# Deformable attention on one Trainium2 core: softmax per 512 queries, maximum subtracted in PSUM, other slots for the small stages

## The chip, the cores and the metric

The kernel runs on one NeuronCore of a Trainium2 chip (trn2). The metric is the device time of one execution in microseconds, here the median of three runs. Engines are named as in the profile: PE (TensorE matmul), PEld (its weight loads), DVE (VectorE), ACT (ScalarE), POOL (GpSimd) and SP (SyncE, which issues the DMAs).

## The reference

Two layers of a block with deformable attention run one after another on x of 2 x 128 x 32 x 32, fp32. Per layer and image:

- q is a grouped 1x1 convolution (8 heads of 16 channels). A 6x6 depthwise convolution with stride 4, gelu and a 1x1 product give 64 sampling positions per head; the image is sampled there bilinearly, and k and v come from the samples.
- The scores of a head are 1024 queries x 64 keys, with a learned bias: for each query and key the signed logarithm of their distance in x and y goes through a small network of 2 -> 32 -> 32 -> 1 with relu.
- softmax over the 64 keys, product with v, output projection and residual, then an MLP of 128 -> 512 -> 128 with gelu and a residual.

```
pos = grid_q[:, :, None, :] - grid_kv[:, None, :, :]
bias = jnp.sign(pos) * jnp.log1p(jnp.abs(pos))
bias = jax.nn.relu(bias @ cpb_w1 + cpb_b1)
bias = jax.nn.relu(bias @ cpb_w2 + cpb_b2)
bias = (bias @ cpb_w3 + cpb_b3).reshape(b, GROUPS, H * W, Hd * Wd)
sim = jnp.einsum('bhid,bhjd->bhij', qh, kh) + bias
attn = jax.nn.softmax(sim, axis=-1)
```

## The kernel before

The work is 4 segments (2 layers x 2 images), each of 4 units (pairs of heads; the 128 partitions are the 2 x 64 keys of a pair), each of 2 phases (512 queries), each of 8 steps. So there are 256 steps, 64 to a segment. The bias network is nearly all of the work.

In a step g, DVE makes the hidden layer for 16 keys x 512 queries (first_layer, L578, one 128x2048 maximum) into one of three buffers. PE does layer 2: 16 products of 32x32 tiles with the distance features (L785, bf16) and 16 with h (L790, fp32, two records each), into two pairs of PSUM banks. ACT applies relu to the two (relu2, L430). PE then does layer 3 of the step before: four products of 128x32 (L802, fp32) that accumulate into the phase's bank of scores. At the second step of a phase scores_start (L806 to L814) begins that bank with the query-key product, one 128x128 product of 512 columns (L812). PSUM holds a ring of three bank pairs, taken in turn by layer 2 and by the small stages, and two single banks of scores, one phase each.

The softmax of a unit, once both its phases are complete: copy_scores (L433, ACT) copies the scores with a bias into probs, per phase; scores_transpose (L884, PE) makes eight 128x128 transposes (L889); score_max (L700, DVE) takes the negative maximum over the 64 keys (L704); widen_max (L513, ACT) repeats it over 64 columns (L519); max_spread (L892, PE) turns it back with eight fp32r products (L896); max_off (L708, DVE) adds it to probs (L711); exp (L522, ACT) is taken in place (L524). Per segment, exp_sums and attend (L907, PE) follow, two DMA round trips and DVE's reciprocal (L715) for the sums, divide, project, residual1, mlp_up (L930) with gelu (L529), mlp_down (L940) and residual2 (L737).

The stages ahead of a segment's attention are norm1, q, the convolution (products on DVE and POOL, L310, sums, gelu), offset, tanh, positions, spread (L859), features, distances (L493, ACT), hats (L672, L675, DVE), hat_products (L681 on DVE, L410 on POOL), sample (L871) and keys_values. They run within the steps of the segment before.

What sets the order is written out by hand: BEFORE_SLOTS, AFTER_SLOTS and SOFTMAX_SLOTS give, for each engine and stage, the step after whose own work the stage is put into that engine's queue, counted from the segment's or unit's start. Each engine runs its queue strictly in order and waits on semaphores. Slots of AFTER_SLOTS count from the start of the next segment, those of BEFORE_SLOTS from the start of the segment before. DVE may be up to three steps ahead of PE (three buffers of h), so a DVE stage at slot s can run while PE is at s - 2. copy_scores has places of its own: after relu2 of slot 12 of the unit, and of slot 0 of the next one.

```
SOFTMAX_SLOTS = {("pe", "scores_t"): 2, ("dve", "score_max"): 3, ("act", "widen_max"): 3, ("pe", "max_spread"): 5,
                 ("dve", "max_off"): 6, ("act", "exp"): 7}
```

## Time and profile before

| what | before |
|---|---|
| time, median of three runs | 993.13 us (992.44 to 996.33) |
| the profiled execution: its time | 995.93 us |
| the profiled execution: its span | 994.1 us, 33269 instructions |
| mean granted PE clock, of full speed | 0.948 |

The span is the time from the first to the last recorded instruction of one execution; the time holds a little around it. PE, DVE and ACT work side by side, so their busy times add up to more than the span. PEclk is the clock that the throttle granted PE: 1.00 is its level of 2.4 GHz, and a mean below it means that a part of the stretch ran at 1.2 GHz.

### The profile page before, as it was taken

The page shows a single profiled execution, that of the slowest core. Times are in us where ns is not written, and L with a number is a line of the kernel's source. Part 1 is how long each engine was busy: PE and PEld are TensorE (multiplying, and loading weights), DVE is VectorE, ACT ScalarE, POOL GpSimd, SP SyncE. Part 2 cuts the span into 40 slices and gives each one's busy share as a digit, 9 for nine tenths or more (in the row PEclk, how much of TensorE's full clock was granted, in tenths as well). Part 3 has the DMA queues.
Part 4 walks back from the last instruction along what each step waited for, and adds up shares of the span by engine and source line. Part 5 has one row for each costly group of instructions (what it writes and reads, how often), then busy time and mean ns, then how long its engine had stood idle before and what let it go on. Part 6 is the DMA issues. An engine that isn't in the chain of part 4 may idle for free.

```text
span 994.1 us, 33269 instructions
## 1 busy us (share of the span) xinstructions
PE 858.1 (86%) x15332; PEld 285.9 (29%) x15332; DVE 727.3 (73%) x473; ACT 639.7 (64%) x710; POOL 61.5 (6%) x40
## 2 busy tenths in 40 slices
PE   2199997789999998779999998879999999999846
PEld 1133322223333322214233332313323333323212
DVE  3679779697887748697978648967978776797511
ACT  1357677757767655856767765666776685687611
POOL 2200002300000002030000002040000000000000
PEclk8589999899999999889999999979999999999958
DMA  3211010020102001002011001002010200100010
GB/s 136 64 40 46 4 45 4 7 48 9 47 3 71 2 2 46 7 1 55 25 25 52 20 1 46 8 2 51 6 47 10 63 2 24 25 3 2 2 45 21
DMA packets 29530, 27.81 MB, mean 28 GB/s; under 512 B 22096, under 2 KB 24016, under 8 KB 29392
## 3 DMA queue, kind: packets, MB, share of 16 engines
q1 hardware_dynamic: 29392, 25.69, 9.9%
q8 instruction: 121, 1.98, 0.8%
q14 instruction: 17, 0.14, 0.0%
HBM read 23.05 MB, written 2.49 MB: 26 GB/s over the span
## 4 chain that ended last, share of the span: by engine, by line
PE 62%; DVE 22%; ACT 8%; issue 4%; DMA 2%; SPq 0%; POOL 0%; ACTq 0%; DVEq 0%; POOLq 0%
PE pair L790 23%; PE scores L802 18%; DVE h L578 12%; PE pair L785 7%; ACT h L430 3%; PE scores L812 3%; PE pair L940 3%; PE pair L930 2%; PE pair L896 1%; DVE probs L711 1%; PE pair L907 1%; DVE big L681 1%; PE pair L889 1%; DVE neg_max L704 1%; DVE big L675 1%
## 5 line engine op out<-in xcount | busy, mean ns | idle before, releaser
L430 ACT ACTIVATE h<-pair 128x1024 f32<-128x1024 f32 x512 | 496.1, 1021 | 256.8 <-PE pair L790 256.7
L578 DVE TENSOR_TENSOR h<-hx,hy 128x2048 f32<-128x2048 f32 x256 | 580.7, 2315 | 3.2 <-PE pair L790 3.0
L790 PE MATMUL pair<-h,wts 32*32 32x512 f32 x8192 | 345.6, 608 | 55.1 <-DVE h L578 55.1
L802 PE MATMUL scores<-h,wts 128*32 128x512 f32 x2048 | 276.0, 611 | 0.9 <-ACT h L430 0.9
L785 PE MATMUL pair<-fy,u_rows 32*32 32x512 bf16 x4096 | 127.9, 388 | 35.0 <-DMA fy<-fy_dram 20.5
L790 PEld LDWEIGHTS pair<-h,wts 32*32 32x32 f32 x8192 | 120.6, 104 | 84.7 <-DVE h L578 72.2
L785 PEld LDWEIGHTS pair<-fy,u_rows 32*32 32x32 bf16 x4096 | 40.4, 88 | 228.9 <-issue 199.8
L802 PEld LDWEIGHTS scores<-h,wts 128*32 128x32 f32 x2048 | 40.8, 108 | 218.2 <-issue 212.5
L704 DVE TENSOR_REDUCE neg_max<-pair 128x16 f32<-128x1024 f32 x16 | 19.5, 1221 | 61.1 <-PE pair L889 61.1
L310 POOL TENSOR_TENSOR conv_prod<-qpad,wts 128x288 f32<-128x288 f32 x16 | 21.6, 1378 | 475.7 <-ACT qpad L456 475.7
L737 DVE SCALAR_TENSOR_TENSOR x<-pair,wts,x 128x1024 f32<-128x1024 f32 x4 | 5.1, 1283 | 57.0 <-PE pair L940 57.0
L410 POOL TENSOR_TENSOR big<-big,hat_x 128x512 f32<-128x512 f32 x16 | 37.1, 2348 | 126.3 <-DVE big L675 126.3
L812 PE MATMUL scores<-qpad,keys_t 128*128 128x512 f32 x64 | 39.2, 697 | 0.0
L711 DVE TENSOR_TENSOR probs<-probs,pair 128x1024 f32<-128x1024 f32 x16 | 19.5, 1219 | 25.1 <-PE pair L896 25.1
L529 ACT ACTIVATE big<-pair,wts 128x1024 f32<-128x1024 f32 x16 | 17.8, 1114 | 27.9 <-PE pair L930 27.9
L930 PE MATMUL pair<-work,wts 128*128 128x512 f32 x64 | 33.9, 663 | 2.2 <-DVE work L731 2.2
L940 PE MATMUL pair<-big,wts 128*128 128x512 f32 x64 | 28.5, 598 | 1.3 <-ACT big L529 1.3
L310 DVE TENSOR_TENSOR conv_prod<-qpad,wts 128x288 f32<-128x288 f32 x16 | 13.9, 915 | 17.0 <-ACT qpad L456 17.0
L439 ACT ACTIVATE probs<-scores,wts 128x512 f32<-128x512 f32 x32 | 22.1, 691 | 1.3 <-PE scores L802 1.3
L493 ACT ACTIVATE big<-work,const 128x512 f32<-128x512 f32 x32 | 20.9, 713 | 0.0
L896 PEld LDWEIGHTS pair<-ident_r,neg_max_wide 128*128 128x128 f32 x128 | 16.3, 200 | 15.7 <-issue 15.7
L896 PE MATMUL pair<-ident_r,neg_max_wide 128*128 128x128 f32 x128 | 18.6, 290 | 2.5 <-ACT neg_max_wide L519 2.5
(90 smaller groups left out, 366.7 us busy)
## 6 DMA issues: line engine op xcount, KB each, us to landing
hx<-features_dram SPq DMA_DIRECT2D x64, 128.0 KB, 2.7
hy<-features_dram SPq DMA_DIRECT2D x64, 128.0 KB, 3.1
att_den<-reciprocals_dram SPq DMA_DIRECT2D x4, 512.0 KB
wts<-weights_dram SPq DMA_DIRECT2D x2, 960.0 KB, 8.4
fy_dram<-fy_part SPq DMA_DIRECT2D x96, 8.0 KB, 1.5
x<-x_dram SPq DMA_DIRECT2D x2, 512.0 KB, 5.8
fy<-fy_dram SPq DMA_DIRECT2D x64, 12.0 KB
out_dram<-x SPq DMA_DIRECT2D x2, 512.0 KB, 5.0
```

The costliest lines, as they stand in the source:

```text
L310: return engine.tensor_tensor(out, window, taps, ALU.mult)
L410: pool.tensor_tensor(bilinear[:, k], hat_y[:, k], hat_x[:], ALU.mult).then_inc(bilinear_ready[0], 1)
L430: emptied("z", 2 * g + j, act.activation(h2[g % H2_BUFS][:, 2 * j:2 * (j + 1)].rearrange("p r n -> p (r n)"), pair_of("z", 2 * g + j)[:], ...
L578: dve.tensor_tensor(h1[g % H1_BUFS][:].rearrange("p c (y x) -> p c y x", x=W), hx[unit % 2][:, :, t].unsqueeze(2).broadcast_to([128, CT, H ...
L704: emptied("scores_t", unit, dve.tensor_reduce(neg_max[:], pair_of("scores_t", unit)[:].rearrange("p (n j) -> p n j", j=NKV), AX_X, ALU.max ...
L785: pe.matmul(z[r][32 * c:32 * (c + 1)], u_rows[l][key[r], 32 * c:32 * (c + 1)], y.unsqueeze(2).broadcast_to([32, H // 2, W]), start=True, s ...
L790: ins = pe.matmul(z[r][32 * c:32 * (c + 1)], w(l, "w2")[key[r], key[r]], h1[g % H1_BUFS][key[r], c], start=False, stop=True)
L802: ins = pe.matmul(scores[phase % 2][32 * r:32 * (r + 1)], w(l, "w3")[:, 32 * t:32 * (t + 1)], h2[g % H2_BUFS][:, r], start=False, stop=t = ...
L812: pe.matmul(scores[phase % 2][:], keys_t[seg % 2][:, u], qpad[seg % 2][:, 1 + H // 2 * h:1 + H // 2 * (h + 1), 1:W + 1], start=True, stop= ...
L896: ins = pe.matmul(pair_of("max_spread", unit)[:, 128 * k:128 * (k + 1)], neg_max_wide[:, 2 * k:2 * (k + 1)].rearrange("p n j -> p (n j)"), ...
L930: ins = pe.matmul(pair_of("mlp_up", n)[:, bank(h)], w(seg // B, "mlp_w1")[:, 128 * c:128 * (c + 1)], xn2[:, bank(h)], start=True, stop=True)
L940: ins = pe.matmul(pair_of("mlp_down", seg)[:, bank(h)], w(seg // B, "mlp_w2")[:, 128 * c:128 * (c + 1)], mlp_h[:, c, bank(h)], start=c == ...
```

## The change

- The softmax runs per phase (512 queries), 32 times, instead of per unit, 16 times. scores are copied once a phase at slot 0 of the next one. The transposes stand at slot 1 (four of them), score_max at slot 3 of DVE, and exp at slot 2 of ACT.
- The maximum is subtracted in PSUM. PE's new stage max_off (slot 2) makes eight fp32 products per phase, each with 64 equal columns of the negative maxima as weights and the 128-column identity as the moving side, which accumulate onto the bank of scores that still holds the phase. exp reads that bank and adds the bias. widen_max, max_spread, DVE's max_off and the one-time cast of the identity to fp32r (L756) are gone.
- scores_start makes four products of 128x32 weights in place of one of 128x128, and waits for exp of the phase before last instead of its copy.
- Most slots of the small stages move. hidden_terms stays at slot 12.

The core of the diff:

```diff
-    ("dve", "norm1", 0): 29, ("pe", "q", 0): 30, ("act", "q_out", 0): 30, ("pool", "conv_products", 0): 31,
+    ("dve", "norm1", 0): 28, ("pe", "q", 0): 28, ("act", "q_out", 0): 28, ("pool", "conv_products", 0): 31,
     ("pool", "conv_products", 1): 31, ("dve", "conv_products", 0): 31, ("dve", "conv_products", 1): 32,
-    ("pe", "image_t", 0): 31, ("act", "image_t_out", 0): 31, ("dve", "conv_sum", 0): 33,
-    ("dve", "conv_sum", 1): 34, ("act", "conv_gelu", 0): 34, ("pe", "offset", 0): 35,
-    ("act", "offset_tanh", 0): 35, ("dve", "positions", 0): 36, ("pe", "spread", 0): 37,
-    ("act", "features", 0): 36, ("act", "spread_out", 0): 37, ("dve", "features_sign", 0): 37,
+    ("pe", "image_t", 0): 30, ("act", "image_t_out", 0): 30, ("dve", "conv_sum", 0): 33,
+    ("dve", "conv_sum", 1): 34, ("act", "conv_gelu", 0): 33, ("pe", "offset", 0): 34,
+    ("act", "offset_tanh", 0): 34, ("dve", "positions", 0): 37, ("pe", "spread", 0): 36,
+    ("act", "features", 0): 36, ("act", "spread_out", 0): 37, ("dve", "features_sign", 0): 39,
     ("act", "distances", 0): 38, ("act", "distances", 1): 39, ("act", "distances", 2): 40,
-    ("act", "distances", 3): 41, ("dve", "hats", 0): 40, ("dve", "hats", 1): 42,
-    ("pool", "hat_products", 0): 40, ("pool", "hat_products", 1): 42, ("dve", "hat_products", 0): 43,
-    ("dve", "hat_products", 1): 44, ("pe", "sample", 0): 46, ("dve", "sample_out", 0): 47,
-    ("pe", "keys_values", 0): 48, ("act", "keys_values_out", 0): 48,
+    ("act", "distances", 3): 41, ("dve", "hats", 0): 42, ("dve", "hats", 1): 44,
+    ("pool", "hat_products", 0): 42, ("pool", "hat_products", 1): 44, ("dve", "hat_products", 0): 45,
+    ("dve", "hat_products", 1): 46, ("pe", "sample", 0): 47, ("dve", "sample_out", 0): 49,
+    ("pe", "keys_values", 0): 50, ("act", "keys_values_out", 0): 50,
...
-    ("pe", "exp_sums", 0): 9, ("act", "exp_sums_out", 0): 9, ("pe", "attend", 0): 10,
-    ("act", "attend_out", 0): 10, ("dve", "reciprocal", 0): 12, ("dve", "divide", 0): 15, ("pe", "project", 0): 16,
-    ("dve", "residual1", 0): 17, ("pe", "mlp_up", 0): 18, ("act", "mlp_gelu", 0): 18, ("pe", "mlp_up", 1): 20,
-    ("act", "mlp_gelu", 1): 20, ("pe", "mlp_up", 2): 22, ("act", "mlp_gelu", 2): 22, ("pe", "mlp_up", 3): 24,
-    ("act", "mlp_gelu", 3): 24, ("pe", "mlp_down", 0): 26, ("dve", "residual2", 0): 27,
+    ("pe", "exp_sums", 0): 3, ("act", "exp_sums_out", 0): 3, ("pe", "attend", 0): 4,
+    ("act", "attend_out", 0): 4, ("dve", "reciprocal", 0): 8, ("dve", "divide", 0): 12, ("pe", "project", 0): 12,
+    ("dve", "residual1", 0): 14, ("pe", "mlp_up", 0): 14, ("act", "mlp_gelu", 0): 14, ("pe", "mlp_up", 1): 15,
+    ("act", "mlp_gelu", 1): 15, ("pe", "mlp_up", 2): 19, ("act", "mlp_gelu", 2): 19, ("pe", "mlp_up", 3): 20,
+    ("act", "mlp_gelu", 3): 20, ("pe", "mlp_down", 0): 22, ("dve", "residual2", 0): 24,
...
-SOFTMAX_SLOTS = {("pe", "scores_t"): 2, ("dve", "score_max"): 3, ("act", "widen_max"): 3, ("pe", "max_spread"): 5,
-                 ("dve", "max_off"): 6, ("act", "exp"): 7}
+SOFTMAX_SLOTS = {("pe", "scores_t"): 1, ("dve", "score_max"): 3, ("pe", "max_off"): 2, ("act", "exp"): 2}
 TERMS_SLOT = 12
-FIRST_COPY = 12
...
-    for unit in range(UNITS):
+    for phase in range(PHASES):
         for (engine, stage), step in SOFTMAX_SLOTS.items():
-            put(engine, UNIT_STEPS * (unit + 1) + step, stage, unit)
+            put(engine, STRIDES * (phase + 1) + step, stage, phase)
...
-            def widen_max(unit):
-                wait_emptied(act, "scores_t", unit)
-                if unit:
-                    wait_filled(act, "max_spread", unit - 1)
-                act.activation(neg_max_wide[:], neg_max[:].unsqueeze(2).broadcast_to([128, 2 * CHUNKS, NKV]), ACT.Copy)\
-                    .then_inc(max_widened, 1)
-            def exp(unit):
-                wait_emptied(act, "max_spread", unit)
-                act.activation(probs[:, unit % PAIRS], probs[:, unit % PAIRS], ACT.Exp).then_inc(exp_ready, 1)
+            def exp(phase):
+                unit, h = phase // 2, phase % 2
+                act.wait_ge(max_taken_off, phase + 1)
+                act.activation(probs[:, unit % PAIRS, bank(h)], scores[phase % 2][:], ACT.Exp, bias=w(unit // PAIRS // B, "b3"))\
+                    .then_inc(exp_ready, 1)
...
-                if g % UNIT_STEPS == FIRST_COPY and g < ALL_STEPS:
-                    copy_scores(2 * (g // UNIT_STEPS))
-                if g and g % UNIT_STEPS == 0 and g <= ALL_STEPS:
-                    copy_scores(2 * (g // UNIT_STEPS) - 1)
+                if g and g % STRIDES == 0 and g <= ALL_STEPS:
+                    copy_scores(g // STRIDES - 1)
...
-            def score_max(unit):
-                wait_filled(dve, "scores_t", unit)
-                if unit:
-                    dve.wait_ge(max_widened, unit)
-                emptied("scores_t", unit, dve.tensor_reduce(
-                    neg_max[:], pair_of("scores_t", unit)[:].rearrange("p (n j) -> p n j", j=NKV), AX_X, ALU.max,
-                    negate=True))
-            def max_off(unit):
-                wait_filled(dve, "max_spread", unit)
-                s = probs[:, unit % PAIRS]
-                emptied("max_spread", unit, dve.tensor_tensor(s, s, pair_of("max_spread", unit)[:], ALU.add))
+            def score_max(phase):
+                wait_filled(dve, "scores_t", phase)
+                if phase >= 2:
+                    dve.wait_ge(max_taken_off, phase - 1)
+                emptied("scores_t", phase, dve.tensor_reduce(
+                    neg_max[phase % 2][:], pair_of("scores_t", phase)[:, 0:HALF].rearrange("p (n j) -> p n j", j=NKV), AX_X,
+                    ALU.max, negate=True))
...
                 if phase >= 2:
-                    pe.wait_ge(scores_copied, phase - 1)
+                    pe.wait_ge(exp_ready, phase - 1)
                 wait_emptied(pe, "keys_values", seg)
-                pe.matmul(scores[phase % 2][:], keys_t[seg % 2][:, u],
-                          qpad[seg % 2][:, 1 + H // 2 * h:1 + H // 2 * (h + 1), 1:W + 1],
-                          start=True, stop=False, skip_group_check=True)
+                for c in range(CT):
+                    k = slice(32 * c, 32 * (c + 1))
+                    pe.matmul(scores[phase % 2][k], keys_t[seg % 2][:, u, k],
+                              qpad[seg % 2][:, 1 + H // 2 * h:1 + H // 2 * (h + 1), 1:W + 1],
+                              start=True, stop=False, skip_group_check=True)
             def turn(stage, n):
...
-            def scores_transpose(unit):
-                pe.wait_ge(scores_copied, 2 * (unit + 1))
-                turn("scores_t", unit)
-                for k in range(CHUNKS):
+            def scores_transpose(phase):
+                unit, h = phase // 2, phase % 2
+                pe.wait_ge(scores_copied, phase + 1)
+                turn("scores_t", phase)
+                for k in range(CHUNKS // 2):
                     s = slice(128 * k, 128 * (k + 1))
-                    ins = pe.transpose(pair_of("scores_t", unit)[:, s], probs[:, unit % PAIRS, s], cst("ident"))
-                filled("scores_t", unit, ins)
-            def max_spread(unit):
-                turn("max_spread", unit)
-                pe.wait_ge(max_widened, unit + 1)
-                for k in range(CHUNKS):
-                    ins = pe.matmul(pair_of("max_spread", unit)[:, 128 * k:128 * (k + 1)],
-                                    neg_max_wide[:, 2 * k:2 * (k + 1)].rearrange("p n j -> p (n j)"),
-                                    ident_r[:], start=True, stop=True)
-                filled("max_spread", unit, ins)
+                    ins = pe.transpose(pair_of("scores_t", phase)[:, s], probs[:, unit % PAIRS, bank(h)][:, s], cst("ident"))
+                filled("scores_t", phase, ins)
+            def max_off(phase):
+                wait_emptied(pe, "scores_t", phase)
+                for k in range(CHUNKS // 2):
+                    for n in range(2):
+                        ins = pe.matmul(scores[phase % 2][NKV * n:NKV * (n + 1), 128 * k:128 * (k + 1)],
+                                        neg_max[phase % 2][:, 2 * k + n:2 * k + n + 1].broadcast_to([128, NKV]),
+                                        cst("ident"), start=False, stop=True, skip_group_check=True)
+                ins.then_inc(max_taken_off, 1)
...
-                pe.wait_ge(exp_ready, PAIRS * (seg + 1))
+                pe.wait_ge(exp_ready, 2 * PAIRS * (seg + 1))
```

## Rows read from the trace of the kernel before

**Rows 1.** The page, part 1: busy us (share of the span) and instructions of each engine.

```profile
PE 858.1 (86%) x15332; PEld 285.9 (29%) x15332; DVE 727.3 (73%) x473; ACT 639.7 (64%) x710; POOL 61.5 (6%) x40
```

**Rows 2.** Busy by stretch: start:end, length, PE, PEld, DVE, ACT, POOL (count), PEclk, DMA share, GB/s.

```profile
60.01:269.77 209.76, 190.41 (x3755) 61.22 (x3751) 177.84 (x115) 149.91 (x169) 15.89 (x8) 0.97 0.10 25
502.41:734.13 231.72, 211.26 (x3837) 69.22 (x3832) 179.33 (x113) 159.21 (x178) 15.87 (x8) 0.98 0.10 25
734.13:920.19 186.06, 178.00 (x3287) 57.88 (x3283) 140.64 (x76) 130.84 (x137) 0.00 (x0) 1.00 0.06 17
```

**Rows 3.** The same view, the second segment cut into five pieces.

```profile
269.77:294.73 24.96, 23.64 (x472) 7.94 (x467) 18.06 (x11) 17.39 (x19) 0.00 (x0) 1.00 0.01 2
294.73:321.31 26.58, 26.58 (x489) 8.14 (x487) 19.90 (x14) 18.58 (x21) 0.00 (x0) 1.00 0.25 66
321.31:390.24 68.93, 62.88 (x965) 20.63 (x960) 46.99 (x28) 44.13 (x45) 5.90 (x4) 1.00 0.07 18
390.24:456.46 66.22, 54.51 (x1015) 18.39 (x1005) 53.75 (x44) 44.82 (x57) 9.98 (x4) 0.90 0.09 21
456.46:502.41 45.95, 44.64 (x919) 14.29 (x917) 40.70 (x21) 34.27 (x39) 0.00 (x0) 1.00 0.14 31
```

**Rows 4.** Timeline of PE: start us, us, engine, line; three steps after a scores_start.

```profile
248.77 1.13 PE L812 MATMUL scores<-qpad,keys_t 128*128 128x512 f32 x2
...
249.82 1.07 PE L802 MATMUL scores<-h,wts 128*32 128x512 f32 x8
...
250.82 0.44 PE L785 MATMUL pair<-fy,u_rows 32*32 32x512 bf16 x16
...
253.31 0.43 PE L785 MATMUL pair<-fy,u_rows 32*32 32x512 bf16 x16
```

**Rows 5.** Timeline of PE around the softmax of one pair, phases 6 and 7.

```profile
228.36 1.09 PE L889 MATMUL pair<-const,probs 128*128 128x128 f32 x8
...
232.97 1.15 PE L790 MATMUL pair<-h,wts 32*32 32x512 f32 x32 [0.66 <-DVE h L578]
...
237.67 1.11 PE L896 MATMUL pair<-ident_r,neg_max_wide 128*128 128x128 f32 x8
```

**Rows 6.** The chain that ended last, in order of time: start us, us, what.

```profile
214.82 1.75 PE pair L871 x64
...
296.85 1.72 PE pair L907 x16
...
334.92 1.91 PE pair L930 x4
...
358.33 7.08 PE pair L940 x16
...
408.79 1.83 PE pair L859 x16
```

**Rows 7.** The same chain in its last stretch, after the last step.

```profile
939.31 0.70 ACT probs L439
...
941.18 1.24 DVE neg_max L704
...
945.62 1.23 DVE probs L711
...
946.87 1.06 ACT probs L524
...
947.98 3.68 PE pair L907 x16
```

**Rows 8.** Timeline of ACT and DVE in the first segment's hat stage.

```profile
182.34 1.93 ACT L430 ACTIVATE h<-pair 128x1024 f32<-128x1024 f32 x2
...
184.29 1.28 ACT L524 ACT_TABLE_LOAD   x1
...
187.90 0.43 DVE L672 TENSOR_SCALAR hat_x<-hat_x 128x512 f32<-128x512 f32 x1 [5.49 <-ACT big L493]
```

**Rows 9.** Groups of DVE by line in 390.24:456.46: xcount, busy us, mean ns, idle before.

```profile
L578 DVE TENSOR_TENSOR h<-hx,hy 128x2048 f32<-128x2048 f32 x18 | 42.6, 2400 | 0.0
```

More of the change, by code:

```diff
@@ L149 @@
 RELEASES = {"spread": 2, "keys_values": 5}
-RING_STAGES = ("u_rows", "q", "image_t", "offset", "spread", "sample", "keys_values", "scores_t", "max_spread", "attend",
+RING_STAGES = ("u_rows", "q", "image_t", "offset", "spread", "sample", "keys_values", "scores_t", "attend",
                "exp_sums", "project", "mlp_up", "mlp_down")
@@ L226, in build @@
         u_rows = [sb(f"u_rows{l}", [128, 128], BF16) for l in range(LAYERS)]
-        neg_max = sb("neg_max", [128, CHUNKS * 2])
-        neg_max_wide = sb("neg_max_wide", [128, CHUNKS * 2, NKV], F32R)
-        ident_r = sb("ident_r", [128, 128], F32R)
+        neg_max = [sb(f"neg_max{k}", [128, CHUNKS]) for k in range(2)]
         probs = sb("probs", [128, PAIRS, HW])
@@ L266, in build @@
         scores_copied = sem("scores_copied")
-        max_widened = sem("max_widened")
+        max_taken_off = sem("max_taken_off")
         exp_ready = sem("exp_ready")
@@ L534, in _ @@
                       "distances": distances, "attend_out": attend_out, "exp_sums_out": exp_sums_out,
-                      "keys_values_out": keys_values_out, "exp": exp, "widen_max": widen_max,
+                      "keys_values_out": keys_values_out, "exp": exp,
                       "mlp_gelu": mlp_gelu}
@@ L750, in _ @@
                       "hat_products": hat_products, "sample_out": sample_out, "hidden_terms": hidden_terms,
-                      "score_max": score_max, "max_off": max_off, "divide": divide, "reciprocal": reciprocal,
+                      "score_max": score_max, "divide": divide, "reciprocal": reciprocal,
                       "residual1": residual1, "residual2": residual2}
@@ L755, in _ @@
             dve.wait_ge(const_loaded, 16)
-            ordered(dve.tensor_copy(ident_r[:], cst("ident")))
             set_up(0)
@@ L944, in _ @@
             stages = {"u_rows": u_of_layer, "q": q, "image_t": image_transpose, "offset": offset, "spread": spread,
-                      "sample": sample, "keys_values": keys_values, "scores_t": scores_transpose, "max_spread": max_spread,
+                      "sample": sample, "keys_values": keys_values, "scores_t": scores_transpose, "max_off": max_off,
                       "attend": attend, "exp_sums": exp_sums, "project": project, "mlp_up": mlp_up, "mlp_down": mlp_down}
```

## The prediction

> **What bounds the kernel now.** I read the busy line first [rows 1]: PE is busy for 86% of the span, DVE for 73%, ACT for 64%. So PE leads, but it idles for 136 us, and two other engines are loaded enough to hold it up. Next the step itself [rows 4]: from one layer-2 start to the next (250.82 to 253.31) PE needs 2.49 us, of which the four w3 products, listed as 1.07, hold 1.00 before the next instruction starts; the listed lengths of back-to-back PE groups overlap by 0.07. A scores_start holds 1.06 (248.77 to 249.82, rounded up). So eight steps with one scores_start are 8 x 2.49 + 1.06 = 21.0 us.
>
> Third, the stretches [rows 3]. I call eight steps a phase. The two phases of a pair in which nothing but its softmax is added take 45.95 us; the plain ones would be 42.0. PE's own part of the extra 3.95 is the transposes and the max products, 1.02 + 1.04 net of the overlap [rows 5]; the other 1.9 is waiting: 0.66 for h in front of layer 2 at 232.97, the same again after max_off, and two slow handovers. DVE has just sat through a 1024-wide reduction or addition, so h is late. The worst stretch is 390.24:456.46 [rows 3], steps 33 to 48 of a segment: 66.2 us. PE's own work in it is two plain phases (42.0), one softmax (2.06), spread 1.83, sample 1.75 [rows 6] and four small products that I estimate at a spread product each (1.83 / 8 = 0.23, together 0.9): 48.6. So 17.6 us are waits and a low clock; PEclk is 0.90 there against 1.00 around it, so part of it ran at the 1.2 GHz level. One wait is visible from the other side: DVE sits 5.49 us until ACT has delivered the distances [rows 8], while no h is made.
>
> Summed for a whole segment with both stages around it: 8 x 21.0 + 4 x 2.06 = 176.2 for steps and softmax; exp_sums and attend 2 x 1.83 (1.72 plus a change of shape, estimated at 0.11), five products of the 1.91 kind and mlp_down 7.08, so 20.3; q another 1.91, image transposes 1.02, spread, sample and the four small ones, 7.4 [rows 5, 6]. That is 204 us, and the second segment took 232.6 [rows 3]: 28.6 lost. By the same sum for each stretch, 17.6 of it lies in steps 33 to 48, 3.8 behind the softmaxes of two other pairs, and 7.2 in steps 17 to 32, where a third softmax stands among mlp and q.
>
> **The change, part by part.**
>
> *scores_start.* One 128x128 product of 512 columns becomes four of 128x32. Rows with both kinds: 32 products of 128x32 and 128 columns end in 1.75, eight of 128x128 take 1.83 [rows 6]; so four column tiles run side by side at about the price of one full product. Eight of 128x32 and 512 columns take 1.72, or 0.86 for four [rows 6]. A group of four that is followed by another shape holds 1.00, a full product followed by 128x32 holds 1.06 [rows 4]. The new group is followed by its own shape, so 0.87: it saves 0.19, 32 times. The Trainium skill ("TensorEngine Tiling (Array Packing)", Key Properties) says that a change of tiling mode drains the array; the rows agree with 0.14 to 0.20 for a change.
>
> *Transposes.* Four per phase in place of eight per pair. Eight hold 1.02 [rows 5]; taking 0.17 of it as the change of shape, four hold 0.59.
>
> *max_off on PE.* New: eight fp32 products per phase, 128x64 weights, 128 columns, two on different column halves. No row shows 64-wide tiles at this length. Bounds: side by side, four rounds of 1.75 / 8 = 0.22 plus a change, 1.03; one after another, eight of 0.23 plus a change, 1.95 [rows 6]. I take 1.03, since the rows with four tiles show full overlap. The same skill page (Restrictions) says that column tiling excludes the fast weight load, which speaks against narrow tiles; by rows 6 narrow fp32 tiles lose nothing to wide ones (1.75 against 1.83), so it changes nothing in the sum.
>
> A phase then holds 21.0 - 0.19 + 0.59 + 1.03 = 22.43 on PE, against (21.0 + 24.95) / 2 = 22.98 now. PE does 1.2 us more per pair, and gains only if the 1.9 of waits goes.
>
> *DVE and ACT.* DVE loses the 1.23 addition; the 1.24 reduction becomes two halves of about 0.70: 1.07 less per pair. ACT loses widen_max and one 1024-wide exp, counted at the 1.06 of exp each, and gets two of 0.70 [rows 7]. Does the order hold? scores_t now stands at the end of step +1, score_max on DVE behind h(+3), max_off on PE at the end of step +2. With PE's step at 2.49, DVE has h(+3) done before scores_t ends, reduces in 0.70 and, with an h at 42.6 / 18 = 2.37 [rows 9], has h(+4) ready 3.1 us after scores_t; PE wants it after 2.49 + 1.03 + 2.49 = 6.0. That slack is why I count the 1.9 as gone. exp waits for max_off behind relu2(+2). relu2 takes 1.93 [rows 8] from the end of layer 2, and PE ends layer 3 and max_off 1.00 + 1.03 after it: the same moment. relu2(+3), queued behind exp, has no product to read for another 1.5, and exp takes 0.70. copy_scores of the odd phases stays where it was; that of the even ones moves from slot 12 to 8 and reads scores whose layer 3 ended 0.9 before relu2 did. max_off uses no ring buffer, so PSUM buffers come free sooner.
>
> *Table loads.* exp now falls between the gelus (slots 14, 18, 19, 26, 33, 34, 36, 42): about four loads more per segment, 1.28 each [rows 8]. Of these two fall in steps 33 to 48. The row ahead of a load ends at 184.27 and the load starts at 184.29: no drain is to be seen. What it would be otherwise is a rival below.
>
> *Steps 33 to 48.* PE: 2 x 22.43 + 1.83 + 1.75 + 0.5 = 48.9. DVE was busy 53.75 [rows 3], with 18 h instead of the 16 that belong here (minus 4.7 [rows 9]), and two halves take the place of a reduction and an addition (minus 1.1): 47.9. ACT: 44.8 [rows 3], plus two loads, minus 0.7 for the softmax and an estimated 1.4 for keys_values_out, which leaves the stretch: 45.3. hats moves two slots behind distances, so the 5.49 goes, and POOL's products start with it, some four steps before sample reads them. But three engines at 93 to 100% of 48.9 do not mesh: ACT falls behind by its two new loads where it also makes the distances (2.6), tanh now waits behind exp and its load, and positions, spread and features behind tanh (0.70 + 1.28 = 2.0); for clock and handovers I add 2.4, my choice. I keep 7 of 17.6. Both ends: 0 and all 17.6. features_sign is two slots later, so the feature and fy stores too; their readers are 20 steps on, and SP waits for nothing new.
>
> *After-stages.* exp_sums to residual2 run 3 to 7 slots earlier. reciprocal has five steps behind exp_sums and divide four behind it, instead of three and three; the round trip over DRAM fits. mlp_down at 22 and residual2 at 24 leave PE two steps in hand; norm1 and q at 28 do too. I count 1.5 us of waits there.
>
> **The sum**, against the profiled execution (span 994.1, time 995.93):
> - second and third segment: 8 x 22.43 + 20.3 + 7.4 = 207.1, plus 8.5 of waits = 215.6, against 232.64 and 231.72 [rows 2, 3]: -17.0, -16.1
> - first: one plain phase at 20.8, seven at 22.43, 7.4, and 9.8 for waits, u_rows and the opening: 195.0 against 209.76 [rows 2]: -14.8
> - fourth, seven phases: 157.0 + 20.3 + 1.0 = 178.3 against 186.06 [rows 2]: -7.8
> - last phase +1.4
> - tail [rows 7]: from the last copy to exp_sums 8.67 now; new 0.70 + 0.59 + 0.70 + 1.03 + 0.70 and handovers, 4.0: -4.7
>
> Together -59.0, so 936.9; the median of the runs lies 2.8 below the profiled execution, which gives 934.
>
> **Rivals.**
> - *max_off in series* (0.13). Its 64-wide tiles take turns: 0.92 more per phase, 32 times, +29: 963. For: nothing shows such tiles side by side. Against: rows 6.
> - *The slots bring nothing* (0.15). Steps 33 to 48 keep 17.6 us of waits, as the three engines are all near full: +10.6 in three segments, +32: 966. For: the loads above. Against: the 5.49 has one clear cause [rows 8].
> - *The softmax chain lies open* (0.04), slower. PE's max_off at step +2 stands ahead of the DVE slot that feeds it, exp holds relu2 behind it. Where DVE has no lead, copy, transposes, reduction, max_off and exp run one after another as in the tail, 4.0 us of which 1.6 is counted: +2.4 in 31 phases, +74: 1008. It decides from 1.9 us per phase on. Against: DVE's load of 40.70 in 45.95 [rows 3].
> - *A switch of tables costs more than its load* (0.02). Where the row before and the row after hide another stop of ACT as long as the load, the four switches in steps 33 to 48 hold ACT 5.1 us longer, 15 in three segments, if all of it reaches PE: 949. Against: the 0.02 us gap [rows 8]. The Trainium skill ("ScalarE: Activation LUTs", What ACT_TABLE_LOAD costs) puts such a drain at 1.38 us on top of 1.28; the trace agrees with the load and shows no drain.
> - *The change does little* (0.02): the waits behind the softmax move elsewhere, and its gain and PE's added work cancel with half the slots' gain: 985 to 995.
>
> **How the numbers follow.** The forecast has 0.64, with its own range 914 (no waits in steps 33 to 48) to 950. To reach 8 in 10 I go up to the two middle rivals: 914 to 966. Within 0.5%, about what a measurement of this kernel can tell from none, is 988 to 998: 0.02; slower 0.04; faster 0.94.
>
> **What would show it.** scores_start groups 0.87 apart from the next w3 products; four transposes about 0.6; max_off 1.0 (1.9 if the rival holds); phases with only a softmax 22.4 long, both alike; no DVE wait in front of hats; steps 33 to 48 near 56. I would be wrong if PE waits in front of max_off for neg_max, or if ACT keeps layer 2 waiting in steps 36 to 44.

## The result and the profile after

The changed kernel takes 930.12 us, median of four runs (929.72 to 933.0), against 993.09 us before: a ratio of 0.937 (95% interval 0.935 to 0.939). The forecast was 934 in a range of 914 to 966. The profiled execution took 930.51 us with a span of 928.7 us.

The page, part 1:

```profile
PE 848.8 (91%) x15908; PEld 300.5 (32%) x15908; DVE 713.9 (77%) x472; ACT 639.5 (69%) x717; POOL 59.9 (6%) x40
```

PE is busy 9 us less than before in a span that is 65 us shorter [rows 1]: its idle time went from 136 to 80 us. Most of that is one wait, the one for h. In page part 5 (busy us, mean ns | idle before it) layer 2 with h stood so before, then so after:

```profile
L790 PE MATMUL pair<-h,wts 32*32 32x512 f32 x8192 | 345.6, 608 | 55.1 <-DVE h L578 55.1
```

```profile
L771 PE MATMUL pair<-h,wts 32*32 32x512 f32 x8192 | 346.6, 597 | 9.7 <-DVE h L565 9.7
```

Lines of the kernel after: L766 and L771 are layer 2 (L785 and L790 before), L783 is layer 3 (L802), L795 scores_start (L812), L873 the transposes (L889), L880 the new max_off, L691 score_max (L704), L565 first_layer (L578).

Busy time by stretch, columns as in [rows 2]: three segments, then the second one cut at the same steps as in [rows 3].

```profile
58.79:255.80 197.01, 190.79 (x3900) 65.50 (x3890) 175.81 (x116) 149.95 (x171) 15.35 (x8) 0.98 0.11 27
...
470.32:683.78 213.46, 208.83 (x3982) 73.67 (x3977) 176.38 (x112) 160.66 (x181) 15.35 (x8) 1.00 0.11 27
...
683.78:860.97 177.19, 177.19 (x3406) 60.46 (x3401) 138.98 (x74) 128.57 (x137) 0.00 (x0) 1.00 0.07 18
...
255.80:281.65 25.85, 25.85 (x514) 8.62 (x509) 19.08 (x10) 18.80 (x21) 0.00 (x0) 1.00 0.11 25
...
281.65:309.81 28.16, 28.16 (x494) 9.61 (x489) 23.01 (x14) 20.27 (x22) 0.00 (x0) 1.00 0.18 42
...
309.81:368.69 58.88, 58.88 (x993) 21.03 (x989) 42.71 (x26) 41.30 (x44) 5.90 (x4) 1.00 0.08 21
...
368.69:424.85 56.16, 51.47 (x1042) 18.84 (x1037) 52.92 (x43) 45.83 (x56) 9.45 (x4) 1.00 0.10 24
...
424.85:470.32 45.47, 45.47 (x961) 15.68 (x956) 38.68 (x21) 34.69 (x42) 0.00 (x0) 1.00 0.15 32
```

The first, third and fourth segments take 197.01, 213.46 and 177.19 us against 209.76, 231.72 and 186.06 [rows 2], the second 214.52 against 232.64. Where the time came from, in the order of [rows 3]: 0.9 more for the first phase, 1.6 more for the next, 10.0 less in steps 17 to 32, 10.1 less in steps 33 to 48, and 0.5 less for the last pair, which now holds two softmaxes of 512 queries. In four of the five stretches PE is busy from end to end.

PE's timeline over the softmax of one phase (start us, us, engine, line):

```profile
860.97 1.07 PE L795 MATMUL scores<-qpad,keys_t 128*32 128x512 f32 x8
861.85 1.04 PE L783 MATMUL scores<-h,wts 128*32 128x512 f32 x8
862.82 0.66 PE L873 MATMUL pair<-const,probs 128*128 128x128 f32 x4
863.41 0.43 PE L766 MATMUL pair<-fy,u_rows 32*32 32x512 bf16 x16
865.90 1.09 PE L880 MATMUL scores<-const,neg_max 128*64 128x128 f32 x16
866.92 0.43 PE L766 MATMUL pair<-fy,u_rows 32*32 32x512 bf16 x16
```

scores_start holds 0.88, the w3 products (layer 3) behind it 0.97, the four transposes 0.59, max_off 1.02 up to the next layer 2. DVE's wait for the transposes and PE's for the maxima are in these groups (page part 5):

```profile
L691 DVE TENSOR_REDUCE neg_max<-pair 128x8 f32<-128x512 f32 x32 | 22.1, 691 | 70.3 <-PE pair L873 70.3
...
L880 PE MATMUL scores<-const,neg_max 128*64 128x128 f32 x512 | 35.0, 279 | 0.8 <-DVE neg_max L691 0.8
```

DVE waits 70.3 us for the transposes in all, where it waited 61.1 for them and another 25.1 for max_spread before. PE waits 0.8 us for neg_max, over all 32 phases, and that wait is the one in the tail. So in no phase but the last does the new softmax hold PE there.

What held PE in steps 33 to 48 of the second segment before (engine line waited for: us in total, times, longest):

```profile
PE pair L790 <- DVE h L578: 8.7, 4, 2.5
PE pair L785 <- ACT h L430: 2.9, 2, 2.6
```

What still holds it:

```profile
PE pair L771 <- DVE h L565: 2.2, 3, 0.7
PE pair L766 <- ACT work L483: 1.9, 1, 1.9
PE pair L766 <- ACT h L426: 0.5, 2, 0.3
```

The chain that ended last, after the last step, against [rows 7]:

```profile
881.50 0.70 ACT probs L435
...
883.68 1.12 PE scores L880 x16
...
884.82 0.69 ACT probs L512
...
885.56 1.97 PE pair L891 x16
...
907.08 8.89 PE pair L914 x16
```

From the last copy to the start of exp_sums it is 4.06 us, against 8.67. exp_sums alone takes 1.97 against 3.68: PEclk over it is 1.00 where it was 0.50, and PE was idle for 0.79 us ahead of it where it was idle for 2.40. The first mlp products, L914, take 8.89 against 10.06 for L930 before, at a PEclk of 0.80 against 0.71. For these the idle time just ahead is the same, 2.23 us, and the one ahead of project is longer, 11.87 against 11.05, so why they ran at the 2.4 GHz level for longer stays open.

### The profile page after: what moved, and what is told of

Read it like the earlier page. It is cut to its first block, busy times and chain, and to the rows that moved or that the text cites. A ratio compares the mean times of both kernels' runs of the same rounds, so it can differ in the third digit from the quotient of the medians.

```text
span 928.7 us, 34427 instructions
## 1 busy us (share of the span) xinstructions
PE 848.8 (91%) x15908; PEld 300.5 (32%) x15908; DVE 713.9 (77%) x472; ACT 639.5 (69%) x717; POOL 59.9 (6%) x40
## 4 chain that ended last, share of the span: by engine, by line
PE 83%; DVE 8%; ACT 3%; DMA 3%; issue 2%; SPq 0%; POOL 0%; ACTq 0%; POOLq 0%; DVEq 0%
PE pair L771 29%; PE scores L783 24%; PE pair L766 9%; PE scores L795 3%; PE pair L914 3%; PE scores L880 3%; DVE h L565 3%; PE pair L924 3%; PE pair L873 2%; ACT h L426 2%; DVE big L668 2%; PE pair L891 1%; PE pair L905 1%; PE pair L818 1%; PE pair L854 1%
## 5 line engine op out<-in xcount | busy, mean ns | idle before, releaser
L565 DVE TENSOR_TENSOR h<-hx,hy 128x2048 f32<-128x2048 f32 x256 | 579.9, 2300 | 41.4 <-PE pair L771 41.1
L771 PE MATMUL pair<-h,wts 32*32 32x512 f32 x8192 | 346.6, 597 | 9.7 <-DVE h L565 9.7
L783 PE MATMUL scores<-h,wts 128*32 128x512 f32 x2048 | 273.6, 606 | 0.9 <-ACT h L426 0.9
L771 PEld LDWEIGHTS pair<-h,wts 32*32 32x32 f32 x8192 | 135.2, 103 | 29.3 <-DVE h L565 13.5
L766 PE MATMUL pair<-fy,u_rows 32*32 32x512 bf16 x4096 | 118.7, 386 | 27.4 <-DMA fy<-fy_dram 20.1
L783 PEld LDWEIGHTS scores<-h,wts 128*32 128x32 f32 x2048 | 43.6, 108 | 209.2 <-issue 208.4
L766 PEld LDWEIGHTS pair<-fy,u_rows 32*32 32x32 bf16 x4096 | 37.6, 88 | 196.7 <-issue 178.4
L691 DVE TENSOR_REDUCE neg_max<-pair 128x8 f32<-128x512 f32 x32 | 22.1, 691 | 70.3 <-PE pair L873 70.3
L880 PEld LDWEIGHTS scores<-const,neg_max 128*64 128x64 f32 x512 | 27.3, 136 | 27.0 <-issue 23.5
L880 PE MATMUL scores<-const,neg_max 128*64 128x128 f32 x512 | 35.0, 279 | 0.8 <-DVE neg_max L691 0.8
L914 PE MATMUL pair<-work,wts 128*128 128x512 f32 x64 | 32.7, 643 | 2.2 <-DVE work L713 2.2
L795 PE MATMUL scores<-qpad,keys_t 128*32 128x512 f32 x256 | 34.1, 605 | 0.0
L512 ACT ACTIVATE probs<-scores,wts 128x512 f32<-128x512 f32 x32 | 22.0, 687 | 8.2 <-PE scores L880 8.0
L435 ACT ACTIVATE probs<-scores,wts 128x512 f32<-128x512 f32 x32 | 22.1, 692 | 1.3 <-PE scores L783 1.3
L873 PEld LDWEIGHTS pair<-const,probs 128*128 128x128 f32 x128 | 13.4, 140 | 27.7 <-issue 26.0
L873 PE MATMUL pair<-const,probs 128*128 128x128 f32 x128 | 21.0, 287 | 0.8 <-ACT probs L435 0.8
```

The lines of the kernel that those rows point to most:

```text
L435: act.activation(probs[:, unit % PAIRS, bank(h)], scores[phase % 2][:], ACT.Identity, bias=w(seg // B, "b3"))\
L565: dve.tensor_tensor(h1[g % H1_BUFS][:].rearrange("p c (y x) -> p c y x", x=W), hx[unit % 2][:, :, t].unsqueeze(2).broadcast_to([128, CT, H ...
L766: pe.matmul(z[r][32 * c:32 * (c + 1)], u_rows[l][key[r], 32 * c:32 * (c + 1)], y.unsqueeze(2).broadcast_to([32, H // 2, W]), start=True, s ...
L771: ins = pe.matmul(z[r][32 * c:32 * (c + 1)], w(l, "w2")[key[r], key[r]], h1[g % H1_BUFS][key[r], c], start=False, stop=True)
L783: ins = pe.matmul(scores[phase % 2][32 * r:32 * (r + 1)], w(l, "w3")[:, 32 * t:32 * (t + 1)], h2[g % H2_BUFS][:, r], start=False, stop=t = ...
L795: pe.matmul(scores[phase % 2][k], keys_t[seg % 2][:, u, k], qpad[seg % 2][:, 1 + H // 2 * h:1 + H // 2 * (h + 1), 1:W + 1], start=True, st ...
```

## Experiments

Times of different groups of runs come with their own runs of the kernel before, so ratios are compared. "Steps 33 to 48" is the stretch between two scores_starts in the second segment: 66.22 before, 56.16 after. The groups had 994.47, 997.36 and 993.82 us for the kernel before. The changed kernel beside the third group:

> The changed kernel once more, so that the others of this group can be compared with it on the same chip: a ratio of 0.937 to the kernel before, and phases as in its first profile.

It took 929.82 us, ratio 0.936 (0.933 to 0.938). Its first and last scores_start lie 802.1 us apart, in the first profile 802.2; I use that distance below too, since prologue and tail drop out of it. Single phases, those of steps 33 to 40 above all, take 1 us more or less from one segment or execution to another. For steps 33 to 40 that is the clock. In the first profile of the changed kernel they take 28.72 in the first segment, at a PEclk of 0.94, and 27.66 in the other two:

```profile
154.19:182.91 28.72, 26.62 (x500) 9.96 (x497) 25.45 (x26) 25.34 (x34) 0.60 (x1) 0.94 0.04 7
368.69:396.35 27.66, 25.44 (x502) 9.74 (x497) 25.45 (x26) 25.23 (x33) 0.60 (x1) 1.00 0.04 7
```

Steps 41 to 48 take 28.50 in the second segment and 27.43 in the others at a PEclk of 1.00; what lengthens those is open.

**The two halves of the change, one at a time.** The new softmax with the old slots of the small stages. The new softmax copies the scores at slot 8 of a segment, and that copy waits for attend, so exp_sums and attend can't go back to 9 and 10; and max_off at slot 26 would wait on DVE behind residual2 at 27, so residual2 went to 28:

```diff
-    ("dve", "norm1", 0): 28, ("pe", "q", 0): 28, ("act", "q_out", 0): 28, ("pool", "conv_products", 0): 31,
+    ("dve", "norm1", 0): 29, ("pe", "q", 0): 30, ("act", "q_out", 0): 30, ("pool", "conv_products", 0): 31,
...
-    ("act", "mlp_gelu", 3): 20, ("pe", "mlp_down", 0): 22, ("dve", "residual2", 0): 24,
+    ("act", "mlp_gelu", 3): 24, ("pe", "mlp_down", 0): 26, ("dve", "residual2", 0): 28,
```

> The changed kernel with the old slots of the small stages (exp_sums and attend stay at 3 and 4, which the new softmax needs; residual2 at 28). Theory (softmax and slots each bring a part): the softmax-only phases stay at 22.4 us, steps 33 to 48 fall back from 56 to about 66 us and steps 17 to 32 lose some 3 us more, so 930 + 30 + 8 = about 968 us. Rival (the old waits in steps 33 to 48 came from the softmax's own 1024-wide steps on DVE): those steps stay below 60 us and the time below 945.

972.22 us, ratio 0.977 (0.974 to 0.980). Phases with only a softmax take 22.4 us, as in the changed kernel. Steps 17 to 32 and 33 to 48:

```profile
318.48:385.75 67.27, 63.09 (x1002) 21.82 (x997) 46.39 (x28) 45.00 (x46) 5.89 (x4) 1.00 0.07 18
385.75:451.04 65.29, 53.91 (x1050) 19.27 (x1041) 52.66 (x44) 45.40 (x58) 10.00 (x4) 0.95 0.08 21
```

65.3 instead of 56.2: as the theory had it, the new softmax alone leaves the stretch nearly as it was (66.2). Steps 17 to 32 are 8.4 longer than in the changed kernel, not 3, of which 3.8 comes back in steps 9 to 16. Then one table of slots at a time: of that edit, only BEFORE_SLOTS (the first two lines and the rest of its table),

> The changed kernel with only the stages ahead of attention at their old slots. Theory (each table of slots pays for itself once the new softmax is in): steps 33 to 48 at 65 us instead of 56, steps 17 to 32 about 2 us longer: 930 + 27 + 6 = about 963 us. Rival (the loss of the kernel with all old slots came from the stages behind attention): below 945.

966.09 us, 0.972 (0.969 to 0.975), and only AFTER_SLOTS:

> The changed kernel with only the stages behind attention at their old slots (exp_sums and attend at 3 and 4, residual2 at 28). Theory: steps 33 to 48 keep their 56 us; mlp_down's last wait comes back and norm1 and q stand close behind it, 3 to 4 us per segment in three: about 941 us. Rival (late mlp stages push the convolution's stages back as well, and steps 33 to 48 grow): above 950.

938.4 us, 0.944 (0.941 to 0.947). The two stretches of the one, then of the other:

```profile
319.44:381.56 62.12, 59.08 (x992) 20.68 (x989) 40.96 (x25) 41.23 (x43) 5.89 (x4) 1.00 0.07 20
381.56:446.83 65.27, 55.77 (x1051) 19.60 (x1041) 53.51 (x44) 45.49 (x58) 9.99 (x4) 0.92 0.09 21
```

```profile
305.41:369.42 64.01, 62.88 (x1002) 22.17 (x997) 44.06 (x29) 45.07 (x47) 9.84 (x4) 1.00 0.07 19
369.42:426.68 57.26, 51.31 (x1040) 18.79 (x1037) 54.41 (x43) 45.96 (x56) 9.47 (x4) 1.00 0.10 23
```

Both theories held (the second costs 938 where I had 941, the first 966 for 963): BEFORE_SLOTS is worth 9.1 us in steps 33 to 48 and 3.2 in steps 17 to 32; AFTER_SLOTS 1.1 and 5.1, of which 3.8 comes back as mlp_up moves into the phase ahead (24.32 there instead of 28.16). The changed kernel's 10.0 less in steps 17 to 32 is in part work of PE that now stands in steps 9 to 16.

The other way round, the old softmax with only the new BEFORE_SLOTS:

> The kernel before with only the new slots of the stages ahead of attention. Theory: the slots take the wait for the distances away by themselves; steps 33 to 48 fall from 66 to about 57 us in three segments, the unit periods stay at 45.95: 993 - 28 = about 965 us. Rival (the slots pay only once DVE and ACT are relieved by the new softmax): above 980.

978.61 us, ratio 0.983 (0.979 to 0.986) against 965 in the theory and above 980 in the rival: between the two, nearer the rival. Steps 33 to 48 stayed at 64.79 where I had expected 57. Why is in the timeline of ACT, PE and DVE:

```profile
399.92 0.61 ACT L487 ACTIVATE work<-pair 128x512 f32<-128x512 f32 x1
...
400.58 1.11 PE L896 MATMUL pair<-ident_r,neg_max_wide 128*128 128x128 f32 x8 [1.89 <-ACT work L487]
...
401.73 1.22 DVE L711 TENSOR_TENSOR probs<-probs,pair 128x1024 f32<-128x1024 f32 x1 [5.43 <-PE pair L896]
```

spread stands at slot 36 and takes a ring buffer, which is free only when ACT's L487 has copied it; the old max_spread (L896) at slot 37 needs that buffer, and DVE's old max_off (L711) waits 5.43 us for max_spread with the next h queued behind it. To test that, spread went back behind max_spread, with nothing else changed:

```diff
-    ("act", "offset_tanh", 0): 34, ("dve", "positions", 0): 37, ("pe", "spread", 0): 36,
+    ("act", "offset_tanh", 0): 34, ("dve", "positions", 0): 37, ("pe", "spread", 0): 37,
```

> The kernel before with the new slots of the stages ahead of attention, but spread on PE back at slot 37, behind max_spread. Theory (with the old softmax the earlier spread takes the ring buffer that max_spread needs, so DVE's max_off waits 5.4 us in place of its old wait for the distances): that wait goes and steps 33 to 48 fall from 65 to about 60 us in three segments, 978.6 - 14 = 965. Rival (the old softmax keeps these steps long in another way): above 974.

966.65 us, ratio 0.968 (0.964 to 0.972); steps 33 to 48 at 60.54, and DVE's waits in them:

```profile
DVE hat_x L672 <- ACT big L493: 1.5, 1, 1.5
DVE probs L711 <- PE pair L896: 0.4, 1, 0.4
```

The wait of 5.4 is 0.4. So in the old kernel BEFORE_SLOTS alone was worth 3.2% with spread behind max_spread and 1.7% in the order of the change. The new softmax takes no ring buffer for the maximum, so spread at 36 can't hold it up; what spread at 37 would do in the changed kernel was not run.

With spread at 37 the two halves nearly add up. The new softmax alone (0.977) times the new BEFORE_SLOTS alone (0.968) is 0.946, and the two together, with the old AFTER_SLOTS, gave 0.944. In steps 33 to 48 the new order saves 5.7 with the old softmax (66.22 to 60.54) and 8.0 with the new one (65.29 to 57.26). Two combinations were not run: the new AFTER_SLOTS with the old softmax, and the softmax split by phase but with the maximum still added by DVE, so what the split and the subtraction in PSUM bring apart from each other is not shown.

**scores_start as one product**, on the changed kernel:

```diff
-                for c in range(CT):
-                    k = slice(32 * c, 32 * (c + 1))
-                    pe.matmul(scores[phase % 2][k], keys_t[seg % 2][:, u, k],
+                pe.matmul(scores[phase % 2][:], keys_t[seg % 2][:, u],
```

> The changed kernel with scores_start as one 128x128 product again. Theory (a change of tile shape is saved): 0.18 us more per phase, 32 times, 5.9 us: 936. Rival (the saving is hidden elsewhere): 930 to 931.

935.29 us, 0.940 (0.936 to 0.943), an interval that overlaps the changed kernel's; the phases decide. Phases with only a softmax take 22.60 or 22.61 instead of 22.41 or 22.42, so 0.19 each as forecast (0.18), and its group holds 1.05 instead of 0.88:

```profile
308.39 1.13 PE L793 MATMUL scores<-qpad,keys_t 128*128 128x512 f32 x2
309.44 1.07 PE L783 MATMUL scores<-h,wts 128*32 128x512 f32 x8
310.44 0.66 PE L871 MATMUL pair<-const,probs 128*128 128x128 f32 x4
```

The scores_starts span 804.0 us in this profile, only 1.8 more than in the changed kernel's first one, and not 31 x 0.19 = 5.9: its first segment has no phase at the lower clock.

**max_off's order.** The eight products by column half, not alternating:

```diff
-                for k in range(CHUNKS // 2):
-                    for n in range(2):
+                for n in range(2):
+                    for k in range(CHUNKS // 2):
```

> The changed kernel with max_off's eight products ordered by column half: four on the lower, then four on the upper. Theory (the two halves run side by side only when they alternate): max_off holds 1.8 to 1.9 us in place of 1.02, 32 times, +28: 958. Rival (its length is set by the weight loads or by issue, so the order does not matter): 930.

942.75 us, ratio 0.947 (0.944 to 0.951). max_off holds 1.51 in place of 1.02:

```profile
318.76 1.58 PE L880 MATMUL scores<-const,neg_max 128*64 128x128 f32 x16
320.27 0.43 PE L766 MATMUL pair<-fy,u_rows 32*32 32x512 bf16 x16
```

The order matters, so the rival is out. But the size was wrong, 0.49 more and not 0.8 to 0.9. The starts of the single records in the two traces show why (each fp32 product leaves two). In the changed kernel they start in pairs, 0.01 us apart, and from pair to pair it is 0.11, 0.82 from the first to the last: the two halves run side by side. By half they fall into two rows of eight, again 0.11 apart within a row, so 0.22 a product, as in the prediction's sum: one from 318.77 to 319.58, the other from 319.26 to 320.07. I take the first for the lower half and the second for the upper. Then the upper half starts while three records of the lower one have yet to start, and the two rows overlap for 0.32 us, so the group grows by 0.49 and not by a whole row's 0.81.

**Three waits that were left.** hidden_terms ahead of the hats:

```diff
-TERMS_SLOT = 12
+TERMS_SLOT = 10
```

> The changed kernel with hidden_terms at slot 10 instead of 12, ahead of the hats. Theory (POOL's hat products slow the two TENSOR_SCALAR of hidden_terms from 1.55 to 3.5 us, and that is why h is late in steps 44 to 46): the two take 1.55 again, the 2.1 us of PE waits for h there go, in three segments: 924 to 925 us. Rival (POOL then slows the h that takes their place, 3.3 in place of 2.28 us, and DVE stays as late): 929 to 930.

927.57 us, ratio 0.929 (0.926 to 0.932); its scores_starts span 799.9 us, 2.3 less. DVE in steps 41 to 46:

```profile
392.14 0.81 DVE L684 TENSOR_SCALAR hx<-hx,wts 128x1024 f32<-128x1024 f32 x1
...
400.68 2.30 DVE L662 TENSOR_SCALAR big<-big 128x2048 f32<-128x2048 f32 x1
...
402.90 3.36 DVE L565 TENSOR_TENSOR h<-hx,hy 128x2048 f32<-128x2048 f32 x1
```

hidden_terms' first half is back at 0.81, but the hats (L662) now take 2.30 instead of 1.21, and one h 3.36. POOL's four hat products, 9.45 in the changed kernel, take 12.11. Both were partly right: the slowdown moves to whatever runs beside POOL, and a smaller part of it is saved. Steps 41 to 48 of the three segments take 26.28, 27.78 and 26.71 for 27.43, 28.50 and 27.43, so 0.7 to 1.2 each of the 2.1 that I expected. spread_out on ACT one slot earlier:

```diff
-    ("act", "features", 0): 36, ("act", "spread_out", 0): 37, ("dve", "features_sign", 0): 39,
+    ("act", "features", 0): 36, ("act", "spread_out", 0): 36, ("dve", "features_sign", 0): 39,
```

> The changed kernel with spread_out on ACT at slot 36, behind features, instead of 37. Theory (the bank pair of spread is freed too late and holds layer 2 of step 38 for 1.9 us): the wait goes in three segments, 924 to 925 us. Rival (relu2 of step 37 is 1.3 us later instead and holds the next layer 2): 928 to 930.

925.64 us, 0.927 (0.924 to 0.930); 795.4 us between the scores_starts, 6.8 less. Steps 33 to 40 take 26.31 in all three segments, for 28.72, 27.66 and 27.66, so the wait accounts for 1.35 in each, 4.1 together. Another 1.06 is the stretch at the lower clock in the first segment, which stood behind that wait and is not there in this profile. The rest, 1.7, is nearly all in steps 17 to 24 of the first segment (25.04 for 26.54), which this edit doesn't touch. In the timeline of the second segment layer 2 of step 38 follows spread_out at once and waits 0.37 for relu2, where it waited 1.89:

```profile
381.74 0.41 PE L766 MATMUL pair<-fy,u_rows 32*32 32x512 bf16 x8 [0.37 <-ACT h L426]
```

Both, and the one-time fy_weights two slots later:

```diff
-    put("dve", 21, "fy_weights", 1)
+    put("dve", 23, "fy_weights", 1)
```

> The changed kernel with hidden_terms at 10, spread_out at 36, and the one-time fy_weights on DVE at 23 instead of 21 (DVE waits 3.8 us for its product there and PE then 1.6 for h). Theory (the three waits are independent): 930 - 5 - 5 - 2.5 = about 918 us, faster than both kernels. Rival (they take each other's place): 925 or more.

> The kernel of three moved slots once more, beside the changed kernel on the same chip. Theory: 0.987 to 0.992 of the changed kernel's time. Rival (its gain was the chip's): 0.997 to 1.003.

921.86 us, ratio 0.924 (0.921 to 0.927); and again 920.86 us, 0.926 (0.923 to 0.929), beside 929.82 for the changed kernel: 0.990. This version is faster than the kernel before and the changed one. 921.86 lies between the theory's 918 and the rival's 925. Its scores_starts span 791.4 us, 10.8 less than in the changed kernel: 5.1 less in the three stretches of steps 33 to 40, 2.4 in those of steps 41 to 48, and 3.3 in steps 17 to 24 of the first segment, where fy_weights stands (23.25 for 26.54; without that edit they took 25.03 when the changed kernel ran again). The steps 17 to 32 and 33 to 48 of its second segment:

```profile
304.27:363.15 58.88, 58.88 (x993) 21.03 (x988) 42.61 (x26) 41.30 (x44) 5.88 (x4) 1.00 0.08 21
363.15:416.97 53.82, 51.35 (x1042) 19.00 (x1037) 53.01 (x43) 45.71 (x56) 12.08 (x4) 1.00 0.11 25
```

## Why the prediction was right, point by point

- *PE's pace and own work.* Right to a hundredth in most terms: scores_start 0.88 (forecast 0.87), transposes 0.59 (0.59), max_off 1.02 (1.03), a softmax-only phase 22.41 (22.43). The bound with the halves side by side was the one to take, and the records of the run by column half show it.
- *The 1.9 us of waits per pair go.* Right: a pair takes 45.47 with 0.65 of keys_values in it, 44.8 without, and PE has no idle time in it. Over the whole kernel PE's wait for h is 9.7 instead of 55.1.
- *Steps 33 to 48.* The total was right, 56.16 against 55.9, and its parts were not; that the total fits is in part luck. I had put 2.6 on ACT's two new table loads, 2.0 on tanh behind exp, 2.4 on clock and handovers. Of these only slow handovers are to be seen. positions starts at 377.68 on DVE without waiting for tanh, which ended at 376.53. PEclk is 1.00 in this segment. The two new loads are there (370.5 and 374.5), but ACT waits for PE again ahead of the next relu2s, so they have been made up. What was measured above my 48.9 is 4.7 of idle time and 2.6 more of busy time. Of the idle time 1.89 is layer 2 of step 38, which needs spread's bank pair; ACT empties it only after features, a table load (381.43) and relu2. That load is an old one; the kernel before has it too (403.31). 2.2 is DVE's lateness in steps 44 to 46, where POOL slows hidden_terms, and 0.5 is relu2. Of the busy time 1.1 is one layer 2 behind sample, listed with 2.41 at 420.02 in place of 1.34, for which I have no cause; the rest is in small delays of 0.1 to 0.3. The step that let POOL's products start with the hats missed that hidden_terms, left at slot 12, now runs beside them: before, it took 0.80 us at 437.78, when POOL had been done since 432.30.
- *My own sign of being wrong came true here.* I had written that I would be wrong if ACT kept layer 2 waiting in steps 36 to 44, and it did, by 1.89 us in step 38. DVE's wait in front of hats, which I had gone, is 1.24 in the second segment, where it was 6.11. Both are small beside the 10.1 us that the stretch gave, so the forecast held in spite of them.
- *Table loads.* The whole kernel has 28 for 21, three more in the second segment where I had counted four.
- *The stages behind attention.* Steps 17 to 32 take 58.88 in place of 68.93. The prediction has no figure for this stretch, but its terms give 2 x 22.43 for the phases, 2 x 1.91 and 7.08 for mlp_up and mlp_down, 1.91 for q and 1.02 for image_t, 58.7, and it counted 1.5 of waits for these stages. Only 0.2 of them is to be seen.
- *The tail.* From copy to exp_sums 4.06 (4.0). The whole tail from the last copy on went from 54.8 to 47.2 us: 7.6 less, not 4.7. exp_sums and the first mlp products, 1.7 and 1.2 shorter in the rows above, make the difference, and both are PE's clock, for which I had priced no change there.
- *The sum.* Against the profiled execution I had 936.9 and it took 930.5, so the sum was 6.4 too high. The tail is 2.9 of that, and the prologue 1.2, which is scatter: the first scores_start comes at 58.79 here, at 60.01 before, and at 59.93 when the same changed kernel ran again. The other 2.3 is in the segments: 197.0 for 195.0, 214.5 and 213.5 for 215.6 twice, 177.2 for 178.3. The first segment came out longer by two stretches at the lower clock (PEclk 0.94 in steps 17 to 24 and 33 to 40). The forecast of 934 lies nearer to the 930.1, because I took 2.8 off for the distance of the profiled execution from the median, which is 0.4 for the changed kernel: that is luck.
- *Rivals.* max_off in series: out. The slots bring nothing: out in the changed kernel (9.1 us per segment from BEFORE_SLOTS), though the old softmax with these slots comes near to that case (64.79 for 66.22). Open chain: out, PE waits 0.8 us in all for neg_max. The change does little: out, the ratio is 0.937. The table switch with a stop beyond its load, as the Trainium skill has it ("ScalarE: Activation LUTs", What ACT_TABLE_LOAD costs): no stop is to be seen here either; relu2 ends at 402.62, the load starts at 402.64, is listed with 1.28, and exp follows at 403.93.

## What to carry to other kernels

When a stage's engine work can only be moved at a price (here PE does 1.2 us more per pair), add up the waits that the old form causes on the engine that sets the end: the 1.9 us of waits were worth more than the work. Hand-set slots belong to the operations that they place: each half of this change gave 2 to 3% alone, and they nearly add up, but only once one stage, spread, had been moved out of the way of the old softmax's ring buffer. In the order of the change the slots gave half as much there. Test a table of slots again whenever a stage stops taking a shared buffer. For narrow products, alternate the column halves: here it is 1.02 against 1.51 us.

## What the runs showed of the hardware that I had not expected

- DVE's two TENSOR_SCALAR of hidden_terms, fp32 from SBUF, take 0.81 and 0.75 us alone and 1.75 and 1.76 beside POOL's TENSOR_TENSOR; an h beside POOL takes 2.88 here and 3.36 in the run with hidden_terms at 10, against 2.28. It goes both ways: POOL's four products take 9.45 us here and 12.11 in that run. The first two rows are from a stretch in which POOL is idle, the last three from one in which it makes the hat products:

```profile
348.47 0.81 DVE L684 TENSOR_SCALAR hx<-hx,wts 128x1024 f32<-128x1024 f32 x1
349.19 0.75 DVE L685 TENSOR_SCALAR hy<-hy,wts 128x1024 f32<-128x1024 f32 x1
```

```profile
399.50 2.88 DVE L565 TENSOR_TENSOR h<-hx,hy 128x2048 f32<-128x2048 f32 x1
402.31 1.75 DVE L684 TENSOR_SCALAR hx<-hx,wts 128x1024 f32<-128x1024 f32 x1
403.99 1.76 DVE L685 TENSOR_SCALAR hy<-hy,wts 128x1024 f32<-128x1024 f32 x1
```

- Fp32 products of 128x64 weights and 128 columns on alternating column halves take 1.02 us for eight with the change of shape, by halves 1.51.
- The same group of four products of 128x32 weights and 512 columns (fp32) holds 0.88 us when its own shape follows (860.97 to 861.85), 0.97 when the transposes do (861.85 to 862.82), and 1.00 when layer 2's 32x32 tiles do [rows 4]: 0.1 for a change of shape. One 128x128 product followed by 128x32 holds 1.05. The Trainium skill ("TensorEngine Tiling (Array Packing)", Key Properties) says that such a change drains the array; the rows agree and put its price here at 0.09 to 0.12 us, up to 0.17 if the full product costs as much as the four narrow ones.
